# Chunk 0's Gram matrices, its pairs and all decay rows, computed head by head in the projection stage

## The chip, the cores and the metric

The kernel runs on one core of one Trainium2 chip. The metric is the device time of one launch in microseconds (us), lower is better. The engines are TensorE (PE, with its weight loads as PEld), VectorE (DVE), ScalarE (ACT), GpSimd (POOL) and SyncE (SP), which here issues every DMA.

## The reference

One transformer layer in fp32, batch 4, 512 steps, 512 channels, 16 heads of 128, cut to what matters:

```python
q = silu(conv(x @ Wq)); k = silu(conv(x @ Wk)) * 128**-0.5; v = silu(conv(x @ Wv))   # causal, 4 taps
a = sigmoid(x @ Wa + ba); beta = sigmoid(x @ Wb + bb)
def step(St, inp):                       # 512 steps, in order, per batch and head
    err = einsum('bhvk,bhk->bhv', St, k_t) - v_t
    St = a_t[..., None] * St - (b_t[..., None] * err)[..., None] * k_t[:, :, None, :]
    return St, einsum('bhvk,bhk->bhv', St, q_t)
o = layernorm(o) * ln_w + ln_b;  o = (o * sigmoid(x @ Wg)) @ Wo
x = layernorm(x + o);  x = layernorm(x + ternary_ffn(x))
```

The recurrence is solved in 16 chunks of 32 steps. A chunk needs the products k·k of its own steps (the Gram matrices, 32 x 32 for each of the 64 pairs of batch and head), of which only the "pairs" within blocks of 8 steps are used, and the decay over the whole chunk, one row of 128 for each pair of batch and head.

## The kernel before

Five stages follow one another with a barrier between them; the change touches the first two.

**Stage 1, `projections`.** x and the weights are split in a high and a low part, and for each head five matrices are multiplied: A (decay), V, Q, K, G (gate), each in 4 tiles of 128 x 512 (one per batch) with 12 matmuls. Tiles rotate through five of the eight PSUM banks. Per head DVE evicts A, waits for ACT's exponential, scales the `ng` tensor by it, and runs three convolutions (`taps_of`, L424) for V, Q, K. The `ng` tensor is first filled by a broadcast load of beta (L166), which SP issues after the last store of the head before. ACT copies the tiles and makes the silus and the gates. POOL multiplies up decays within blocks of 8 steps (21 steps, semaphore `s_pr`); its last products are `r_out`. DVE splits the weights' low parts (`split`, L419); when the fifth is split (`s_wlo`), SP may load the weights of the next head but one (`weights`, L158). SP works strictly in the order of its list: ng, A, r (2 stores), vt, q, weights, g, k, and then the beta load of the next head. All outputs go to DRAM scratch tensors.

**Stage 2, `recurrence`.** Each of 16 chunks is a cycle. DVE solves a triangular system in 4 blocks for 2 halves of the 64 pairs of batch and head (`solve`, L1173), with `cross` and `start` between. POOL multiplies the pairs by the gates (`with_gates`, L779), masks the key products, decays the state UT (`decay`, L767; needs the decay rows `crow`), rescales X and subtracts v from W (`less_v`). PE transposes X and multiplies. The numbers T_... and D_... are places in a fixed order of the PSUM banks. For chunk c+1 the Gram matrices are made during cycle c: PE `gram` (L984), ACT `copy_gram`, SP `write_gram` to DRAM, then `compact` (7 DRAM to DRAM copies that pick the pairs), then `load_gb` (broadcast to all partitions). Chunk 0 has no cycle before it, so the same chain runs at the head of the stage (L695 to L711, L945 to L953, L1126 to L1141), together with the transposition of all decays into `crow` rows and the first state products, whose state is zero.

**Stages 3 to 5** are the output projection, the ternary weights and the feed-forward net.

Of the kernel before, what the change touches and what calls it, by code (L numbers as in the profile page):

```python
# [5 lines left out]
F32 = mybir.dt.float32  # L6
# [5 lines left out]
P = 128  # L12
# [4 lines left out]
CH = 32  # L17
# [41 lines left out]
def projections(nc, x, w_mats, ba, wb, bb, conv_w, conv_b, scr):  # L59
# [10 lines left out]
    with ExitStack() as ctx:  # L70
# [37 lines left out]
        s_zero = m.sem("zero")  # L108
# [3 lines left out]
        s_exp = m.sem("exp")  # L112
# [6 lines left out]
        s_st = {n: m.sem(f"st_{n}") for n in ("q", "k", "ng", "vt", "A", "g", "r")}  # L119
# [15 lines left out]
        def _(sp):  # L135
# [4 lines left out]
            sp.wait_ge(s_zero, 1)  # L140
# [22 lines left out]
            def head(h, first, left):  # L163
# [9 lines left out]
                store("ng")  # L173
                sp.wait_ge(s_pr, N_PR * (h + 1))
# [4 lines left out]
                sp.wait_ge(s_vt, h + 1)  # L179
                store("vt")  # L180
                sp.wait_ge(s_silu, 3 * h + 2)
                store("q")
# [13 lines left out]
            for n in s_st:  # L196
                sp.wait_ge(s_st[n], (32 if n == "r" else 16) * NH)

        @block.gpsimd
        def _(pool):  # L200
            make_identity(nc, pool, ident, s_id)
            nc.gpsimd.memset(w_in[:, 0, :, :], 0.0).then_inc(s_zero, 1)
            for i in range(2):
                nc.gpsimd.memset(y[i][:, :, 0:KW - 1], 0.0).then_inc(s_zero, 1)
# [9 lines left out]
            def head(h, first):  # L214
# [12 lines left out]
                pool.wait_ge(s_a, h + 1)  # L227
# [36 lines left out]
        def _(act):  # L264
# [18 lines left out]

            def head(h, first, more):
# [31 lines left out]
                nc.scalar.activation(ra[:, :, :], av[:, :, :], ACT.Exp, scale=-1.0).then_inc(s_exp, 1)  # L316
                act.wait_ge(s_exp, h + 1)
                nc.scalar.activation(av[:, :, :], av[:, :, :], ACT.Sigmoid).then_inc(s_a, 1)  # L318
                split(A)
                rows(V)  # L320
                rows(Q)
                silu(V)
                rows(K)
                silu(Q, "q")
                if not first:
                    act.wait_ge(s_st["g"], 16 * h)
                for b in range(B):
                    act.wait_ge(s_mm, TILES * h + PER_MAT * G + b + 1)
                    nc.scalar.activation(outs["g"][:, :, b, :], bank[PER_MAT * G + b][:, :].rearrange("p (c t) -> p c t", t=CH), ACT.Sigmoid).then_inc(s_g, 1)
                split(G)  # L330
                silu(K, "k")
# [7 lines left out]
        def _(pe):  # L339
# [24 lines left out]
            def head(h, first):  # L364
                for mat in range(5):
                    pe.wait_ge(s_wlo, 5 * h + mat + 2)
                    for b in range(B):
# [12 lines left out]
                        product(bank[j][:, :], mat, b).then_inc(s_mm, 1)  # L380

            head(0, True)
            with pe.Fori(1, NH) as h:
                head(h, False)

        @block.vector
        def _(dve):
# [30 lines left out]
            def head(h, first, more):  # L418
# [5 lines left out]
                def taps_of(mat):  # L424
# [5 lines left out]
                    if mat == V:  # L430
                        dve.wait_ge(s_zero, 3)
# [14 lines left out]
                dve.wait_ge(s_exp, h + 1)  # L446
# [27 lines left out]
def weight_piece(views, i, j):  # L474

    return views[i][:, 4 * j:4 * j + 4, :] if i < 2 else views[i][:, j, :, :]


def recurrence(nc, scr, mats, wo, part, res, first):
# [17 lines left out]
    with ExitStack() as ctx:  # L497
# [26 lines left out]
        s_mask = m.sem("mask")  # L524
# [5 lines left out]
        s_cr = m.sem("cr")  # L530
# [25 lines left out]
        T_START, T_CH = 12, 32  # L556
# [18 lines left out]
        all_decays = Gm[:, :, :, :, :].rearrange("p g a i t -> p (g a i t)").rearrange("p (c x) -> p c x", c=NCH)  # L575
        decay_rows = crow[0:HB, 0:NCH, :]
# [12 lines left out]
        def _(sp):  # L589
# [1417 lines left out]
```

## Time and profile before

| | us |
|---|---|
| device time, median of 3 (lowest, highest) | 2773.33 (2772.25, 2779.79) |
| the profiled execution | 2769.04 |
| its span, first to last instruction | 2767.3 |
| PE busy in the span | 2549.2 (92%) |
| DVE busy | 2034.7 (74%) |
| POOL busy | 1415.3 (51%) |
| ACT busy | 1163.7 (42%) |

Stage 1 takes the first 937 us, the recurrence runs from there to about 2022 us. The profiled execution is 1.7 us longer than its span (launch and end) and 4.3 us shorter than the median. Matmul times overlap, so PE's share says how often it had work, not how close it is to its peak.

### The profile page before, as it was taken

The page shows a single profiled execution, that of the slowest core. Times are in us where ns is not written, and L with a number is a line of the kernel's source. Part 1 is how long each engine was busy: PE and PEld are TensorE (multiplying, and loading weights), DVE is VectorE, ACT ScalarE, POOL GpSimd, SP SyncE. Part 2 cuts the span into 40 slices and gives each one's busy share as a digit, 9 for nine tenths or more (in the row PEclk, how much of TensorE's full clock was granted, in tenths as well). Part 3 has the DMA queues.
Part 4 walks back from the last instruction along what each step waited for, and adds up shares of the span by engine and source line. Part 5 has one row for each costly group of instructions (what it writes and reads, how often), then busy time and mean ns, then how long its engine had stood idle before and what let it go on. Part 6 is the DMA issues. An engine that isn't in the chain of part 4 may idle for free. (4 is left out here: it accounts for less than half of the span.)

```text
span 2767.3 us, 50124 instructions
## 1 busy us (share of the span) xinstructions
PE 2549.2 (92%) x17682; PEld 2204.6 (80%) x17682; DVE 2034.7 (74%) x5890; ACT 1163.7 (42%) x2265; POOL 1415.3 (51%) x1213
## 2 busy tenths in 40 slices
PE   8999999999999579999999999999858997899999
PEld 6888878888888569888888888889747776788887
DVE  4777677767777369899999999999769885333333
ACT  4454445444544322222322223323578774333333
POOL 2643554355335489889999988999502220000000
PEclk9999999999999889999999999999869999999999
DMA  5466556555555666555555565566755544000000
GB/s 134 130 164 171 165 144 162 171 168 144 161 168 167 190 240 230 209 199 199 218 200 201 203 232 225 218 235 221 280 205 197 197 167 159 33 11 11 11 11 15
DMA packets 417317, 454.35 MB, mean 164 GB/s; under 512 B 122496, under 2 KB 367232, under 8 KB 393856
## 3 DMA queue, kind: packets, MB, share of 16 engines
q1 hardware_dynamic: 417152, 452.22, 48.7%
q8 instruction: 95, 1.56, 0.2%
q14 instruction: 70, 0.57, 0.1%
HBM read 321.49 MB, written 131.14 MB: 164 GB/s over the span
## 5 line engine op out<-in xcount | busy, mean ns | idle before, releaser
L355 PE MATMUL pa_ps<-pa_x_hi,pa_w_hi 128*128 128x512 f32 x1296 | 508.7, 393 | 10.0 <-ACT pa_y L298 5.6
L355 PE MATMUL pa_ps<-pa_x_lo,pa_w_hi 128*128 128x512 f32 x1296 | 506.0, 390 | 0.0
L355 PE MATMUL pa_ps<-pa_x_hi,pa_w_lo 128*128 128x512 f32 x1296 | 505.7, 390 | 0.0
L438 DVE SCALAR_TENSOR_TENSOR pa_cv<-pa_y,pa_taps,pa_cv 128x2048 f32<-128x2048 f32 x144 | 356.4, 2475 | 17.8
L1188 DVE TENSOR_TENSOR pb_tmp<-pb_gb,pb_ps 128x112 f32<-128x112 f32 (+6 forms) x1792 | 328.8, 222 | 23.6 <-POOL pb_gb L786 19.3
L1193 DVE TENSOR_TENSOR pb_ps<-pb_ps,pb_tmp 128x112 f32<-128x112 f32 (+6 forms) x1792 | 331.2, 227 | 0.0
L786 POOL TENSOR_TENSOR pb_gb<-pb_gb,pb_ng 128x448 f32<-128x448 f32 (+6 forms) x448 | 319.3, 754 | 6.6 <-DMA pb_gb<-scratch_pairs 3.5
L355 PEld LDWEIGHTS pa_ps<-pa_x_hi,pa_w_hi 128*128 128x128 f32 x1296 | 244.2, 188 | 68.6 <-ACT pa_y L298 10.4
L770 POOL TENSOR_TENSOR all_res<-all_res,pb_crow 128x1024 f32<-128x1024 f32 x120 | 282.2, 2363 | 21.2 <-DMA pb_crow<-scratch_crow 21.2
L355 PEld LDWEIGHTS pa_ps<-pa_x_hi,pa_w_lo 128*128 128x128 f32 x1296 | 244.3, 188 | 51.3
L355 PEld LDWEIGHTS pa_ps<-pa_x_lo,pa_w_hi 128*128 128x128 f32 x1296 | 244.4, 189 | 50.0
L1031 PE MATMUL pb_ps<-pb_Gm,pb_XT 128*128 128x64 f32 (+1 forms) x2048 | 251.4, 280 | 6.3 <-DVE all_res L1221 3.1
L1031 PEld LDWEIGHTS pb_ps<-pb_Gm,pb_XT 128*128 128x128 f32 x2048 | 245.2, 198 | 11.6 <-issue 5.9
L225 POOL TENSOR_TENSOR pa_o_vt<-pa_av 128x256 f32<-128x256 f32 x16 | 11.6, 728 | 464.5 <-ACT pa_av L318 464.5
L851 ACT ACTIVATE pb_XT<-pb_ps 128x512 f32<-128x512 f32 x256 | 142.9, 595 | 234.9 <-PE pb_ps L981 234.8
L1006 PE MATMUL pb_ps<-pb_kq,all_res 128*128 128x64 f32 x2048 | 239.6, 277 | 0.0
L1006 PEld LDWEIGHTS pb_ps<-pb_kq,all_res 128*128 128x128 f32 x2048 | 236.6, 195 | 0.7
L873 ACT ACTIVATE pb_Gm<-pb_ps 128x256 f32<-128x256 f32 (+1 forms) x256 | 77.3, 354 | 334.0 <-PE pb_ps L997 334.0
L981 PE MATMUL pb_ps<-pb_ident,pb_X 128*128 128x128 f32 x1024 | 150.6, 287 | 71.9 <-DVE pb_X L1201 55.3
L1898 DVE SCALAR_TENSOR_TENSOR pe_hid<-pe_ps,all_scales,pe_sil 128x512 f32<-128x512 f32 x64 | 48.1, 751 | 227.9 <-ACT pe_sil L1782 227.9
L981 PEld LDWEIGHTS pb_ps<-pb_ident,pb_X 128*128 128x128 f32 x1024 | 115.7, 146 | 95.9 <-DVE pb_X L1201 78.1
L452 DVE SCALAR_TENSOR_TENSOR pa_o_ng<-pa_ra,pa_o_ng 128x512 f32<-128x512 f32 x64 | 72.9, 1197 | 129.4 <-DMA pa_o_ng<-scratch_beta 129.4
(192 smaller groups left out, 5364.8 us busy)
## 6 DMA issues: line engine op xcount, KB each, us to landing
pb_crow<-scratch_crow SPq DMA_DIRECT2D x30, 2048.0 KB, 10.2
pb_gb<-scratch_pairs SPq DMA_DIRECT2D x64, 896.0 KB, 8.2
pa_o_ng<-scratch_beta SPq DMA_DIRECT2D x16, 1024.0 KB, 7.9
scratch_ng<-pa_o_ng SPq DMA_DIRECT2D x16, 1024.0 KB, 4.5
scratch_A<-pa_o_A SPq DMA_DIRECT2D x16, 1024.0 KB, 4.5
scratch_vt<-pa_o_vt SPq DMA_DIRECT2D x16, 1024.0 KB, 4.5
scratch_q<-pa_o_q SPq DMA_DIRECT2D x16, 1024.0 KB, 6.9
scratch_g<-pa_o_g SPq DMA_DIRECT2D x16, 1024.0 KB, 8.1
```

What stands on the lines that cost most here:

```text
L355: last = nc.tensor.matmul(out, w[:, mat, k, :], xx[:, k, b * S:(b + 1) * S], start=(k == 0 and n == 0), stop=(k == KT - 1 and n == 2))
L438: nc.vector.scalar_tensor_tensor(out=out, in0=yy[:, :, k:k + S], scalar=tap(k), in1=out, op0=ALU.mult, op1=ALU.add).then_inc(s_tap, 1)
L452: last = nc.vector.scalar_tensor_tensor(out=out, in0=tile(ra, b), scalar=-1.0 / DV, in1=out, op0=ALU.mult, op1=ALU.mult)
L770: tt(uu, uu, crow[:, 8 * (e % 4):8 * (e % 4) + 8, :], ALU.mult).then_inc(s_us, 1)
L786: last = tt(pairs, pairs, ng[:, :, BL * n + t:BL * n + t + 1].broadcast_to([P, HB, w]), ALU.mult)
L851: nc.scalar.activation(out, psT[j % 2][:, :].rearrange("p (g k) -> p g k", g=4), ACT.Copy).then_inc(s_te, by)
L873: last = nc.scalar.activation(Gm[:, g:g + 4, a, :, steps], src[:, :, 1 - a, :, part], ACT.Copy)
L981: last = nc.tensor.transpose(bank[:, q * P:(q + 1) * P], src, ident[:, :])
L1006: last = nc.tensor.matmul(bank[:, 64 * q:64 * q + 64].rearrange("p (a t) -> p a t", a=2), UT[:, 8 * j + q, :], kq[p][:, :, 8 * j + q, :], ...
L1031: last = nc.tensor.matmul(bank[:, 64 * q:64 * q + 32 * kinds].rearrange("p (a i t) -> p a i t", i=4, t=BL), XT[:, g, :], Gm[:, g, 0:kinds, ...
L1188: tt(tmp[:, hs, 0:w], gb[n][:, hs, off[t]:off[t] + w], ys[:, qs, t:t + 1].broadcast_to([P, QUART, w]), ALU.mult).then_inc(s_sv, 1)
L1193: tt(ys[:, qs, t + 1:BL], ys[:, qs, t + 1:BL], tmp[:, hs, 0:w], ALU.add).then_inc(done, 1)
```

## The change

In stage 1, Q and K change places: K is now the third matrix and Q the fourth, and the stores likewise (k early, q last). Behind the fifth matrix of each head PE multiplies the 4 Gram matrices of chunk 0 for this head and transposes its decays of all chunks (`grams`), into a sixth PSUM bank; ACT copies both out (`gram_out`) and SP stores them (`store_gram`, `store_decays`). In the last head this happens ahead of the last tile, and SP also runs the compaction of chunk 0 there. The recurrence then starts with loads alone. The decay rows lie in DRAM by head and then by chunk, so that a load of half of them reads 8 runs per partition instead of one. The zero fills of the state and of the first half of W, O and y are made by DVE, in place of POOL's fill and of the first products with the zero state; PE's bank counter starts at 4 instead of 12. The file also renames a few semaphores (`s_exp`, `s_zero` and `s_mask` are folded into others).

```diff
@@ projections: SP
+                def store_gram():
+                    sp.wait_ge(s_gk, 2 * h + 2)
+                    sp.dma_start(scr["gram"][0, 0:CH * HB * CH].rearrange("(j h x) -> h j x", j=CH, h=NH)[h, :, :], gk[0:CH, 0:P]).then_inc(s_st["gram"], 16)
+                def store_decays():
+                    sp.dma_start(scr["crow"][h, :, :, :].rearrange("c b v -> (c b) v"), gk[:, P:2 * P]).then_inc(s_st["gram"], 16)
+                if left == 0:
+                    sp.wait_ge(s_silu, 3 * h + 2)
+                    store("k")
                 sp.wait_ge(s_pr, N_PR * (h + 1))
                 store("A")
...
+                if left == 0:
+                    store_gram()
+                    sp.wait_ge(s_vt, h + 1)
+                    store("vt")
+                    sp.wait_ge(s_st["gram"], 32 * NH - 16)
+                        compact_pairs(sp, scr, 0, s_st["gram"])
+                if left:
+                    sp.wait_ge(s_vt, h + 1)
+                    store("vt")
+                    sp.wait_ge(s_silu, 3 * h + 2)
+                    store("k")
                 if left >= 2:
                     weights(h + 2)
                 sp.wait_ge(s_g, 4 * h + 8)
                 store("g")
+                if left:
+                    store_gram()
+                store_decays()
                 sp.wait_ge(s_silu, 3 * h + 3)
-                store("k")
+                store("q")
@@ projections: GpSimd
+                    pool.wait_ge(s_gr, h)
@@ projections: ScalarE
+            def gram_out(h, first):
+                act.wait_ge(s_gr, h + 1)
+                if not first:
+                    act.wait_ge(s_st["gram"], 32 * h)
+                nc.scalar.activation(gk[0:CH, 0:P], gram[0:CH, 0:P], ACT.Copy).then_inc(s_gk, 1)
+                nc.scalar.activation(gk[:, P:2 * P], gram[0:NCH * B, P:2 * P], ACT.Copy).then_inc(s_gk, 1)
@@ projections: TensorE
+            def grams(h, first):
+                pe.wait_ge(s_pr, N_PR * (h + 1))
+                pe.wait_ge(s_silu, 3 * h + 2)
+                if not first:
+                    pe.wait_ge(s_gk, 2 * h)
+                for b in range(B):
+                    k = outs["k"][:, 0, b, :]
+                    nc.tensor.matmul(gram[0:CH, CH * b:CH * (b + 1)], k, k, start=True, stop=True)
+                decays = r_out[:, 1, :, :, NBL - 1].rearrange("p c b -> p (c b)")
+                nc.tensor.transpose(gram[0:NCH * B, P:2 * P], decays, ident[:, :]).then_inc(s_gr, 1)
...
                         product(bank[j][:, :], mat, b).then_inc(s_mm, 1)
+                        if mat == G and b == (B - 1 if more else B - 2):
+                            grams(h, first)
@@ recurrence: SP
-                sp.dma_start(flat(crow[:, :, :]), scr["crow"][c, HALF * hf:HALF * (hf + 1), :].rearrange("h v -> (h v)").partition_broadcast(P)).then_inc(s_crl, 16)
+                sp.dma_start(crow[:, :, :].rearrange("p (h b) v -> p h (b v)", b=B),
+                             scr["crow"][NH // 2 * hf:NH // 2 * (hf + 1), c, :, :].rearrange("h b v -> h (b v)").partition_broadcast(P)).then_inc(s_crl, 16)
@@ recurrence: GpSimd
-            nc.gpsimd.memset(UT[:, :, :], 0.0).then_inc(s_te, 4)
-            nc.gpsimd.memset(O[1][:, :, :], 0.0).then_inc(s_os[1], 16)
+            nc.gpsimd.memset(O[1][:, 0:1, :], 0.0).then_inc(s_os[1], 16)
...
-            for hf in range(2):
-                masked(8 + 2 * hf + 1, 0, hf)
             with_gates(0, 0)
+            masked(1, 0, 0)
             with_gates(0, 1)
+            masked(3, 0, 1)
@@ recurrence: VectorE
-            for j in range(4):
-                start(D_START - D_CH, 0, j, 3 if j == 3 else 1)
+            nc.vector.memset(UT[:, 0:HALF, :], 0.0).then_inc(s_dp, 6)
+            nc.vector.memset(UT[:, HALF:HB, :], 0.0).then_inc(s_te, 4)
+            nc.vector.memset(W[:, 0:HALF, :], 0.0)
+            nc.vector.memset(O[0][:, 0:HALF, :], 0.0)
+            nc.vector.memset(y_of[0], 0.0).then_inc(s_de, 6)
             first_v(D_START - D_CH, 0, 0)
```

`compact_pairs` is the old body of `compact`, moved out so that both stages call it. In DVE's list of stage 1 the convolution of K takes the place of Q's, and Q's the last place.

**SP in the loop over heads of stage 1**, from the store of vt to the end of the body. Before:

```order
L170 DMA scratch_vt<-pa_o_vt 128x16x128
L170 DMA scratch_q<-pa_o_q 128x16x128
L161 DMA pa_w_in<-in_Wa 128x4x128
L161 DMA pa_w_in<-in_Wv 128x4x128
L161 DMA pa_w_in<-in_Wq 128x4x128
L161 DMA pa_w_in<-in_Wk 128x4x128
L161 DMA pa_w_in<-in_Wg 128x4x128
L170 DMA scratch_g<-pa_o_g 128x16x128
L170 DMA scratch_k<-pa_o_k 128x16x128
```

Now:

```order
L172 DMA scratch_vt<-pa_o_vt 128x16x128
L172 DMA scratch_k<-pa_o_k 128x16x128
L163 DMA pa_w_in<-in_Wa 128x4x128
L163 DMA pa_w_in<-in_Wv 128x4x128
L163 DMA pa_w_in<-in_Wk 128x4x128
L163 DMA pa_w_in<-in_Wq 128x4x128
L163 DMA pa_w_in<-in_Wg 128x4x128
L172 DMA scratch_g<-pa_o_g 128x16x128
L178 DMA scratch_gram<-pa_gk 32x128
L181 DMA scratch_crow<-pa_gk 64x128
L172 DMA scratch_q<-pa_o_q 128x16x128
```

Two small stores now stand between the store of g and the last store of the head, and so ahead of the beta load that opens the next pass.

**SP from the last head into the recurrence.** Before (the last two stores, the barrier at L70, and the chain of chunk 0):

```order
L170 DMA scratch_g<-pa_o_g 128x16x128
L170 DMA scratch_k<-pa_o_k 128x16x128
L70 UNCONDITIONAL_BRANCH
L588 UNCONDITIONAL_BRANCH
L591 DMA pb_kq<-scratch_k 128x2048
L591 DMA pb_kq<-scratch_q 128x2048
L599 DMA pb_rr<-scratch_r 128x256 x2
L697 DMA pb_Gm<-scratch_r 128x16x256
L607 DMA scratch_gram<-pb_gst 32x512 x4
L591 DMA first_A<-scratch_vt 128x2048
L619 DMA scratch_pairs<-scratch_gram 256x1x7
```

Now, from the end of the compaction in the last head:

```order
L537 DMA scratch_pairs<-scratch_gram 256x1x1
L172 DMA scratch_g<-pa_o_g 128x16x128
L181 DMA scratch_crow<-pa_gk 64x128
L172 DMA scratch_q<-pa_o_q 128x16x128
L70 UNCONDITIONAL_BRANCH
L646 UNCONDITIONAL_BRANCH
L677 DMA pb_gb<-scratch_pairs 128x1792
L649 DMA pb_ng<-scratch_ng 128x2048
L649 DMA first_A<-scratch_vt 128x2048
L649 DMA pb_kq<-scratch_k 128x2048
L649 DMA pb_kq<-scratch_q 128x2048
L657 DMA pb_rr<-scratch_r 128x256 x2
```

The seven compaction copies stand ahead of the barrier (L70), and the first load behind it is that of the pairs (`gb`); k and q come fourth and fifth.

**PE at the head of the recurrence.** Before:

```order
L989 MATMUL pb_ps<-pb_kq 32x32 x64
L1006 MATMUL pb_ps<-pb_kq,all_res 128x64 x32
L1137 MATMUL pb_ps<-pb_ident,pb_Gm 64x128 x16
L997 MATMUL pb_ps<-pb_kq 128x128 x16
L981 MATMUL pb_ps<-pb_ident,pb_X 128x128 x8
```

Now:

```order
L1039 MATMUL pb_ps<-pb_kq 128x128 x16
L1023 MATMUL pb_ps<-pb_ident,pb_X 128x128 x8
L1039 MATMUL pb_ps<-pb_kq 128x128 x4
L1073 MATMUL pb_ps<-pb_Gm,pb_XT 128x64 x8
L1039 MATMUL pb_ps<-pb_kq 128x128 x4
L1031 MATMUL pb_ps<-pb_kq 32x32 x48
```

The Gram products (L989), the state products (L1006) and the transposes of the decays (L1137) are gone from here; the key products (now L1039) come first. The last row, the Gram matrices of chunk 1, waits for chunk 1's k and q.

## Rows read from the trace of the kernel before

**Rows 1.** The page, part 5: a convolution step of DVE, busy us and mean ns.

```profile
L438 DVE SCALAR_TENSOR_TENSOR pa_cv<-pa_y,pa_taps,pa_cv 128x2048 f32<-128x2048 f32 x144 | 356.4, 2475 | 17.8
```

**Rows 2.** Waits of PE in stage 1: us in total, times, longest.

```profile
PE pa_ps L355 <- ACT pa_y L298: 5.6, 9, 0.8
```

**Rows 3.** Timeline of DVE, one head: start us, us, instruction, idle before.

```profile
822.97 2.72 DVE L444 TENSOR_SCALAR pa_av<-pa_ps,pa_ba_sb 128x512 f32<-128x512 f32 x4
...
839.15 4.87 DVE L452 SCALAR_TENSOR_TENSOR pa_o_ng<-pa_ra,pa_o_ng 128x512 f32<-128x512 f32 x4 [8.84 <-DMA pa_o_ng<-scratch_beta]
...
878.15 2.72 DVE L444 TENSOR_SCALAR pa_av<-pa_ps,pa_ba_sb 128x512 f32<-128x512 f32 x4
```

**Rows 4.** Timeline of SP, the same head.

```profile
823.22 0.40 SPq L161 DMA_DIRECT2D pa_w_in<-in_Wa  x1
...
826.23 0.40 SPq L170 DMA_DIRECT2D scratch_g<-pa_o_g  x1
826.81 3.82 SPq L170 DMA_DIRECT2D scratch_k<-pa_o_k  x1
830.84 2.78 SPq L166 DMA_DIRECT2D pa_o_ng<-scratch_beta  x1
```

**Rows 5.** Windows, that head: engines' busy us, PEclk, DMA share, GB/s.

```profile
828.00:829.00 1.00, 1.00 (x6) 0.84 (x5) 0.00 (x0) 1.00 (x1) 0.00 (x0) 1.00 0.86 229
...
831.00:832.00 1.00, 1.00 (x6) 0.84 (x5) 0.00 (x0) 1.00 (x1) 0.00 (x0) 1.00 1.14 346
```

**Rows 6.** Timeline of PE: decay transposes, and Gram products of a later chunk.

```profile
959.62 1.14 PE L1137 MATMUL pb_ps<-pb_ident,pb_Gm 128*64 128x128 f32 x8 [0.24 <-ACT pb_crow L950]
...
998.25 1.20 PE L989 MATMUL pb_ps<-pb_kq 128*32 128x32 f32 x32
```

**Rows 7.** Timeline, end of stage 1 and first load of the recurrence.

```profile
916.93 0.30 POOL L256 COPY pa_r_out<-pa_r_out 128x64 f32<-128x64 f32 x1
...
917.26 0.37 SPq L170 DMA_DIRECT2D scratch_A<-pa_o_A  x1
...
917.67 3.94 SPq L177 DMA_DIRECT2D scratch_r<-pa_r_out  x2
...
930.23 0.39 SPq L170 DMA_DIRECT2D scratch_k<-pa_o_k  x1
...
937.10 0.35 SPq L591 DMA_DIRECT2D pb_kq<-scratch_k  x1
```

**Rows 8.** Timeline, head of the recurrence.

```profile
938.16 6.92 POOL L739 MEMSET all_res<- 128x8192 f32 x1
...
954.75 6.51 SPq L619 DMA_DIRECT2D scratch_pairs<-scratch_gram  x7
...
963.75 3.88 POOL L765 TENSOR_TENSOR pb_Gm<-pb_Gm,pb_mask 128x512 f32<-128x512 f32 x4 [13.19 <-ACT pb_Gm L873]
...
971.17 9.89 POOL L786 TENSOR_TENSOR pb_gb<-pb_gb,pb_ng 128x448 f32<-128x448 f32 x14 [3.54 <-DMA pb_gb<-scratch_pairs]
...
976.23 0.45 DVE L1188 TENSOR_TENSOR pb_tmp<-pb_gb,pb_ps 128x112 f32<-128x112 f32 x2 [16.33 <-POOL pb_gb L786]
...
981.00 1.82 POOL L777 TENSOR_TENSOR pb_W<-pb_W,first_A 128x768 f32<-128x768 f32 x1
...
982.63 2.07 PE L997 MATMUL pb_ps<-pb_kq 128*128 128x128 f32 x8
...
989.18 0.45 DVE L1188 TENSOR_TENSOR pb_tmp<-pb_gb,pb_ps 128x112 f32<-128x112 f32 x2
...
1002.39 0.45 DVE L1188 TENSOR_TENSOR pb_tmp<-pb_gb,pb_ps 128x112 f32<-128x112 f32 x2 [2.94 <-POOL pb_gb L786]
```

**Rows 9.** Window of the first loads (columns as in rows 5).

```profile
940.00:945.00 5.00, 0.00 (x0) 0.00 (x0) 0.00 (x0) 0.00 (x0) 5.00 (x1) 0.50 1.01 400
```

**Rows 10.** DMA issues of 900 to 1010 us: KB each, median us to landing.

```profile
scratch_gram<-pb_gst SPq DMA_DIRECT2D x8, 64.0 KB, 2.1
```

**Rows 11.** Waits of POOL from the recurrence on.

```profile
POOL all_res L770 <- DMA pb_crow<-scratch_crow: 21.2, 14, 6.6
```

More of the change, by code:

```diff
@@ L178, in head @@
                                  r_out[:, i, :, :, :].rearrange("p n b k -> p n (b k)")).then_inc(s_st["r"], 16)
[L179 to L182, printed above, removed]
+                if left == 0:
[3 more added lines that the diff above has]
+                    sp.wait_ge(s_st["gram"], 32 * NH - 16)
+                    with nc.allow_non_contiguous_dma(reason="compaction to the pairs, chunk 0"):
+                        compact_pairs(sp, scr, 0, s_st["gram"])
[4 more added lines that the diff above has]
+                    store("k")
                 if left >= 2:
@@ L327, in head @@
                 for b in range(B):
+                    if b == B - 1 and not more:
+                        gram_out(h, first)
                     act.wait_ge(s_mm, TILES * h + PER_MAT * G + b + 1)
                     nc.scalar.activation(outs["g"][:, :, b, :], bank[PER_MAT * G + b][:, :].rearrange("p (c t) -> p c t", t=CH), ACT.Sigmoid).then_inc(s_g, 1)
+                if more:
+                    gram_out(h, first)
                 split(G)
-                silu(K, "k")
+                silu(Q, "q")
             head(0, True, True)
@@ L362, in _, with head @@
             pe.wait_ge(s_beta, B)
-            def head(h, first):
+            def grams(h, first):
[8 more added lines that the diff above has]
+                nc.tensor.transpose(gram[0:NCH * B, P:2 * P], decays, ident[:, :]).then_inc(s_gr, 1)
+            def head(h, first, more):
                 for mat in range(5):
@@ L476, in weight_piece, with compact_pairs @@
     return views[i][:, 4 * j:4 * j + 4, :] if i < 2 else views[i][:, j, :, :]
+def compact_pairs(sp, scr, c, sem):
+    row = HB * CH
+    off = [sum(BL - 1 - i for i in range(j)) for j in range(BL)]
+    for j in range(BL - 1):
+        first = j * row + j + 1
+        src = scr["gram"][c, first:first + NBL * (BL * row + BL)].rearrange("(n s) -> n s", n=NBL)[:, 0:row]
+        sp.dma_start(scr["pairs"][c, :, :, off[j]:off[j + 1]],
+                     src.rearrange("n (h t) -> n h t", t=CH)[:, :, 0:BL - 1 - j]).then_inc(sem, 16)
 def recurrence(nc, scr, mats, wo, part, res, first):
@@ L612, in compact @@
                 for k in range(2):
-                    sp.wait_ge(s_gw[k], 32 * (c + 1))
-                row = HB * CH
+                    sp.wait_ge(s_gw[k], 32 * c)
                 with nc.allow_non_contiguous_dma(reason="compaction to the pairs, once per chunk"):
-                    for j in range(BL - 1):
-                        first = j * row + j + 1
-                        src = scr["gram"][c, first:first + NBL * (BL * row + BL)].rearrange("(n s) -> n s", n=NBL)[:, 0:row]
-                        sp.dma_start(scr["pairs"][c, :, :, off[j]:off[j + 1]],
-                                     src.rearrange("n (h t) -> n h t", t=CH)[:, :, 0:BL - 1 - j]).then_inc(s_gc, 16)
+                    compact_pairs(sp, scr, c, s_gc)
             def load_gb(c, n):
```

126 lines of the change are left out of this document (52 added, 74 removed).

## The prediction, made before the changed kernel ran

> **What bounds the kernel now.** I read the timeline of each engine over one head of stage 1, then the waits, the windows of the DMA engines, and the timeline across the barrier into the recurrence.
>
> In stage 1 PE looks like the bound, but in at least nine of the sixteen heads it waits 0.6 us for a tile that ACT could not yet copy (5.6 us in 9 waits) [rows 2]. So something else sets the pace by a small margin. DVE shows what: it begins two heads 55.18 us apart (822.97 and 878.15), and between them it stands idle for 8.84 us until the beta load for `ng` lands; from 839.15 to the next head it is never free for long [rows 3]. SP shows why the load is late. It may load weights only when DVE has split the fifth matrix, at about 823. Then come five weight loads, the store of g at 826.23, the store of k at 826.81 and the beta load at 830.84 [rows 4]. So the loop is: 39.0 us of DVE (839.15 to 878.15), then 16.2 us of SP's list and the DMA engines (822.97 to 839.15). At its head the DMA engines are short of work (229 GB/s at 828), afterwards full (346 GB/s at 831) [rows 5].
>
> At the end of stage 1 the last store is issued at 930.23 and the recurrence opens at 937.10 [rows 7]. I call 937.10 S. From there DVE waits until 976.23, S+39.1, for the pairs of chunk 0, which POOL multiplies from 971.17 [rows 8]. The whole chain of Gram matrices, stores and compaction lies ahead of that. The second block begins at S+52.1 (989.18), the third at S+65.3 (1002.39) [rows 8].
>
> **The change, part by part.**
>
> *PE in stage 1.* Sixteen Gram products took 1.20 us (32 records, two for each), so four are 0.30 us; eight transposes took 1.14 us, so one is 0.14 [rows 6]. That is 0.44 us a head, 7.1 in all. PE's waits of 0.6 us cover it as long as the DVE loop sets the pace [rows 2]. I take 0, with 0 and 7 as bounds. The new wait for POOL's products costs nothing in the loop. In the last head POOL ends at 917.2 [rows 7], and the Gram products stand behind the third G tile; what they hold up is one tile's gate, while DVE's convolution runs until some 2 us before the last store. ACT's two copies lie in its idle time.
>
> *Two small stores in SP's list.* They stand before the last store of the head and thus before the beta load. Issue to issue is 0.58 us (826.23 to 826.81) [rows 4], so two cost SP 1.16 us. But SP's next store is then held up by full queues (3.82 us), and g's 1 MB keeps the engines fed meanwhile. Only their 48 KB are certain: 0.14 us at 346 GB/s [rows 5]. Since the engines are not quite full just there, I take 0.25 us a head, 3.5 us over the 14 passes through this loop; the bounds are 2 and 16.
>
> *The end of stage 1.* K's 1 MB now leaves before A's store, which takes 3.0 us of backlog away (1 MB at 346). But SP must do this in order: r's two stores until 921.6 [rows 7], the Gram store, then wait for its landing, 2.1 us when little is queued [rows 10] and some 4 us behind A and r, so about 926. Seven compaction copies took 6.51 us [rows 8]; I count 5 to 6.5. Then g, the decays and q at 0.58 each: q is issued at 932.5 to 934 in place of 930.23. With two full stores still to move (6.1 us at 346) the barrier opens at about 940. I take +3, bounds 0 and +6.
>
> *The head of the recurrence.* Loads run at 400 GB/s [rows 9], with some 2.5 us before the first lands. The order is gb (0.9 MB), ng, vt, k, q (1 MB each), rr, gb, crow (2 MB), two gb, and chunk 1's k and q, 12.3 MB in all. So ng lands at S+7.4, q at S+15.3, crow at S+23.5 and chunk 1's q at S+33.
> - POOL, now without the fill of 6.92 us [rows 8], starts the gates at S+7.4. Half of 9.89 us later [rows 8], at S+12.4, the pairs are ready.
> - DVE fills 10,496 elements per partition. No row has a DVE fill; POOL's took 0.84 ns an element [rows 8], a convolution step on DVE 1.21 ns [rows 1]. That gives 8.9 to 12.7 us and with y minus v a start at S+10.3 to S+14.1. I take S+12.8, near POOL's rate. Solving takes 4.5 us, to S+17.3.
> - PE's four key products wait for q. Four of them as at 982.63, 2.07 us each, are 8.3 us [rows 8]; that was after an idle stretch. The granted clock is 0.50, the lower level of 1.2 GHz, over the first loads, when PE has done nothing for a while, and 1.00 amid stage 1 [rows 5, 9]. At the low level they end at S+23.6, at the full one (half the time) at S+19.5; I take S+22. The rest of the step (12.95 us from solve to solve, less 4.5 for the solve) is 8.4 us: S+30.4.
> - POOL masks the first half behind the key products (half of 3.88 us, to S+22), makes the second gates (4.95, S+27), masks again (1.9) and subtracts v (1.82) [rows 8]: S+30.8. DVE adds this in 0.4 and begins block 2 at about S+31.3, against S+52.1.
> - Then POOL's list up to the third gates is as before, 19.6 us from 982.8 (981.00 + 1.82), of which some 6.6 were the wait for crow [rows 11], which now lies in SBUF. So the third block starts near S+43.9 in place of S+65.3. PE's Gram products of chunk 1 wait for S+33 and delay it by about 1 us.
>
> The gain is thus 21 to 21.4 us at these points, 20.5 with PE's lateness. Lower bound 16: everything at 346 GB/s, the slow clock and the slow fill. Upper bound 22.
>
> The Trainium skill, "DMA: Bandwidth & Descriptors", section "Where 436 GB/s comes from", puts the limit of one core's HBM at about 358 GB/s. By that limit 12.3 MB would take 34.4 us in place of 30.8, and the gain would be about 18 us. The window shows 400 [rows 9], so the sum stays with the row.
>
> *Decay rows in 2 KB runs.* Rows show 346 GB/s for runs of 512 bytes and 400 for long ones [rows 5, 9], so a load of 2.1 MB grows by at most 0.8 us. POOL waited 14 times for crow, 21.2 us in all [rows 11], but PE makes it wait behind that as well, and DVE does not wait for it. I take +1 in all, bounds 0 and 12.
>
> **The sum**, against the profiled execution of 2769.04: -20.5 + 3.5 + 3 + 1 = -13.0, that is 2756. The median of the runs shown is 4.3 above that execution, 2773.33, so I forecast 2760.
>
> **The rivals.**
>
> *A: SP's issue time is paid in full.* For it: SP's list is the loop's link, and the engines run short at 828 [rows 5]. Against: the store behind is held up for 3.82 us anyway [rows 4]. 1.16 x 14 = 16.2 us in place of 3.5, so 2773: no change. Chance 0.14.
>
> *B: the gain at the head is smaller, or PE's products are not hidden.* If PE stays at the low clock and chunk 1's loads come late, the gain is 13 and the time 2768; if the 7.1 us of PE are paid, 2767. For it: PE has idled before and the list puts k and q fourth and fifth. Against: before, POOL and not PE set the third block [rows 8]. Chance 0.15.
>
> *C: slower. Each small store holds up the beta load by its full landing time*, 2.1 us [rows 10]. Place: between g and q in SP's list, each head. Price: 4.2 x 14 = 59 us in place of 3.5, so 2816. It decides as soon as a head grows by over 1.2 us (16.5 us over 14 heads); past 1.8 us it is measurably slower. For it: this list is the bound. Against: SP does not wait for a landing there, and other stores overlap. Chance 0.09. Beside it stands a rule of the Trainium skill, "DMA: Bandwidth & Descriptors", section "Anatomy of one DMA": a DMA has a fixed cost of some 2.0 us whatever its size. The landing of 2.1 us for 64 KB agrees with it, and the same section puts most of that in the completion, which would not add up here.
>
> *The forecast*, stage 1 growing by little and 17 to 22 us won at the head: 0.62.
>
> **How the numbers follow.** What a measurement of this kernel can tell is about 0.3%, 8.3 us, so 2765 and 2782 divide the cases. The forecast case lies from 2751 to 2765, B mostly within 0.3%, A within, C above. That gives faster 0.63, same 0.27, slower 0.10. The range 2750 to 2776 holds the forecast, B and A and leaves out C and the ends of both sides, some 0.18.
>
> **What would show it.** Right: the distance between two heads on DVE at 55.3 to 55.6 us; PE's waits in stage 1 shorter than 0.6; the barrier 5 to 8 us later than 937.1; the first solve at 12 to 15 us behind the first load of the recurrence, the second block at 30 to 33, the third at 43 to 46; crow waits of POOL 0.5 us longer in each chunk, and chunks as long as before. Wrong: a distance of 56.3 or more between heads (A, C), POOL or PE late in the first chunk (B), or a compaction that ends after 933 at the end of stage 1.

## The result: 2821 us, slower by about 2%

| | median us (lowest, highest; runs) | ratio to before, 95% interval |
|---|---|---|
| before, beside it | 2772.79 (2771.44, 2779.79; 4) | |
| changed | 2821.10 (2815.41, 2835.01; 4) | 1.0205 [1.0166, 1.0244] |

2760 with 2750 to 2776 was predicted. The quotient of the two medians alone is 1.0174, inside the interval. That the kernel is slower is clear; whether by 2% is open. The profiled execution is the slowest of the four, 2835.01 us with a span of 2833.3, against 2769.04 for that of before. So the traces differ by 66 us where the medians differ by 48.

The timeline up to the recurrence reads almost as predicted. DVE, two heads of stage 1 (as in [rows 3]):

```profile
825.10 2.72 DVE L495 TENSOR_SCALAR pa_av<-pa_ps,pa_ba_sb 128x512 f32<-128x512 f32 x4
...
880.85 2.72 DVE L495 TENSOR_SCALAR pa_av<-pa_ps,pa_ba_sb 128x512 f32<-128x512 f32 x4
```

The distance is 55.75 us in place of 55.18; the last head begins 2.7 us later than before. SP at the end of the stage (as in [rows 7]):

```profile
925.30 0.89 SPq L178 DMA_DIRECT2D scratch_gram<-pa_gk  x1
...
928.67 5.26 SPq L537 DMA_DIRECT2D scratch_pairs<-scratch_gram  x7
...
936.91 0.59 SPq L172 DMA_DIRECT2D scratch_q<-pa_o_q  x1
943.22 0.34 SPq L677 DMA_DIRECT2D pb_gb<-scratch_pairs  x1
```

S is now 943.22, 6.1 us later. The head of the recurrence (as in [rows 8]):

```profile
944.14 3.47 DVE L1293 MEMSET all_res<- 128x4096 f32 x1 [13.22 <-PEq L70]
...
950.64 4.97 POOL L833 TENSOR_TENSOR pb_gb<-pb_gb,pb_ng 128x448 f32<-128x448 f32 x7 [2.51 <-DMA pb_ng<-scratch_ng]
...
955.72 0.45 DVE L1219 TENSOR_TENSOR pb_tmp<-pb_gb,pb_ps 128x112 f32<-128x112 f32 x2 [0.81 <-POOL pb_gb L833]
...
958.31 5.91 PE L1039 MATMUL pb_ps<-pb_kq 128*128 128x128 f32 x32 [32.44 <-DMA pb_kq<-scratch_q]
...
973.87 0.45 DVE L1219 TENSOR_TENSOR pb_tmp<-pb_gb,pb_ps 128x112 f32<-128x112 f32 x2
...
981.32 1.91 PE L1031 MATMUL pb_ps<-pb_kq 128*32 128x32 f32 x32 [12.12 <-DMA pb_kq<-scratch_q]
...
993.36 0.45 DVE L1219 TENSOR_TENSOR pb_tmp<-pb_gb,pb_ps 128x112 f32<-128x112 f32 x2
```

Gates at S+7.4, solve at S+12.5, second block at S+30.7: all three as in the sum. Only then something is late: chunk 1's q is there at S+38.1 in place of S+33, and the third block at S+50.1 in place of S+43.9. The windows say why. While the decay rows load, the DMA engines move less (columns as in rows 5):

```profile
960.00:965.00 5.00, 4.83 (x31) 4.59 (x31) 0.25 (x1) 2.40 (x9) 2.27 (x3) 0.73 0.74 244
965.00:970.00 5.00, 4.21 (x36) 3.92 (x35) 0.75 (x2) 2.23 (x6) 5.00 (x8) 1.00 0.63 153
```

The same loads in `e1_rows_by_chunk` (below), where the decay rows lie in one run, keep their rate:

```profile
955.00:960.00 5.00, 4.81 (x35) 4.49 (x34) 0.16 (x1) 2.71 (x9) 2.42 (x3) 0.82 0.98 414
960.00:965.00 5.00, 3.69 (x33) 3.50 (x32) 0.75 (x2) 1.91 (x5) 5.00 (x8) 1.00 1.02 423
```

All 30 loads of the decay rows are slow. DMA issues (KB each, median us to landing), before and after:

```profile
pb_crow<-scratch_crow SPq DMA_DIRECT2D x30, 2048.0 KB, 10.2
```

```profile
pb_crow<-scratch_crow SPq DMA_DIRECT2D x30, 2048.0 KB, 16.7
```

These medians hide a pattern. Before, the loads land alternately after some 8.6 and 13.6 us, and the median falls between the two; in the changed kernel both kinds take 15 to 19 us (the first 25). By the mean without the first load the growth is from 10.9 to 16.6 us. POOL's wait for them grew from 21.2 us [rows 11] to 130.3. Waits of POOL, and one of them on its timeline:

```profile
POOL all_res L817 <- DMA pb_crow<-scratch_crow: 130.3, 24, 9.9
```

```profile
1018.41 2.36 POOL L817 TENSOR_TENSOR all_res<-all_res,pb_crow 128x1024 f32<-128x1024 f32 x1 [9.93 <-DMA pb_crow<-scratch_crow]
```

A chunk can be measured by ACT's instruction that occurs once in each. First and last after:

```profile
993.91 0.61 ACT L972 ACTIVATE pb_ngx<-pb_ng 128x512 f32<-128x512 f32 x1
...
2025.88 0.64 ACT L972 ACTIVATE pb_ngx<-pb_ng 128x512 f32<-128x512 f32 x1
```

That is 1031.97 us for 15 distances, 68.8 us each; before (L925, from 1000.04 to 1960.72) they are 64.05. So the account of the profiled executions is: the first of these instructions comes 6.1 us earlier than before, 15 x 4.75 = 71.3 us are lost, and the last comes 65.2 us later; under 1 us of the 66 lies behind it. The surprise is in the chunks and in 6 us of the head, both behind the loads of the decay rows.

### The profile page after: what moved, and what is told of

The parts are those of the page before. It is cut to its first block and busy times, and to the rows that moved or that the text cites. A ratio compares the mean times of both kernels' runs of the same rounds, so it can differ in the third digit from the quotient of the medians.

```text
span 2833.3 us, 50183 instructions
## 1 busy us (share of the span) xinstructions
PE 2599.8 (92%) x17618; PEld 2253.7 (80%) x17618; DVE 2041.6 (72%) x5883; ACT 1166.3 (41%) x2289; POOL 1398.4 (49%) x1212
## 5 line engine op out<-in xcount | busy, mean ns | idle before, releaser
L817 POOL TENSOR_TENSOR all_res<-all_res,pb_crow 128x1024 f32<-128x1024 f32 x120 | 282.3, 2364 | 130.3 <-DMA pb_crow<-scratch_crow 130.3
L391 PEld LDWEIGHTS pa_ps<-pa_x_lo,pa_w_hi 128*128 128x128 f32 x1296 | 244.2, 188 | 50.1
L1073 PE MATMUL pb_ps<-pb_Gm,pb_XT 128*128 128x64 f32 (+1 forms) x2048 | 263.7, 288 | 21.1 <-issue 9.3
L1073 PEld LDWEIGHTS pb_ps<-pb_Gm,pb_XT 128*128 128x128 f32 x2048 | 257.4, 206 | 28.1 <-issue 20.6
L1048 PE MATMUL pb_ps<-pb_kq,all_res 128*128 128x64 f32 x1984 | 254.6, 293 | 0.0
L1048 PEld LDWEIGHTS pb_ps<-pb_kq,all_res 128*128 128x128 f32 x1984 | 252.5, 211 | 0.6
L248 POOL TENSOR_TENSOR pa_o_vt<-pa_av 128x256 f32<-128x256 f32 x16 | 11.7, 730 | 473.8 <-ACT pa_av L350 473.8
L1039 PE MATMUL pb_ps<-pb_kq 128*128 128x128 f32 x1024 | 163.1, 309 | 39.7 <-DMA pb_kq<-scratch_q 32.4
## 6 DMA issues: line engine op xcount, KB each, us to landing
pb_crow<-scratch_crow SPq DMA_DIRECT2D x30, 2048.0 KB, 16.7
```

The lines of the kernel that those rows point to most:

```text
L391: last = nc.tensor.matmul(out, w[:, mat, k, :], xx[:, k, b * S:(b + 1) * S], start=(k == 0 and n == 0), stop=(k == KT - 1 and n == 2))
L817: tt(uu, uu, crow[:, 8 * (e % 4):8 * (e % 4) + 8, :], ALU.mult).then_inc(s_us, 1)
L1039: last = nc.tensor.matmul(bank[:, q * P:(q + 1) * P].rearrange("p (a i t) -> p a i t", a=2, i=4), flat(kq[p][:, 0, 4 * g:4 * g + 4, :]), k ...
L1048: last = nc.tensor.matmul(bank[:, 64 * q:64 * q + 64].rearrange("p (a t) -> p a t", a=2), UT[:, 8 * j + q, :], kq[p][:, :, 8 * j + q, :], ...
L1073: last = nc.tensor.matmul(bank[:, 64 * q:64 * q + 32 * kinds].rearrange("p (a i t) -> p a i t", i=4, t=BL), XT[:, g, :], Gm[:, g, 0:kinds, ...
```

## The experiments

The chunk times below are means over the first 14 of these distances unless said otherwise; after has 68.75 by this measure. Landing is the median of the 30 loads of the decay rows.

**Is it the layout?** `e1_rows_by_chunk` is the changed kernel with the decay rows in DRAM by chunk, one run of 16 KB for each partition; each head's store then scatters its rows.

```diff
-sp.dma_start(scr["crow"][h, :, :, :].rearrange("c b v -> (c b) v"), gk[:, P:2 * P])
+sp.dma_start(scr["crow"].rearrange("c (g b) v -> g c b v", b=B)[h, :, :, :], gk[:, P:2 * P])
...
```

The tensor's shape and the load are those of the kernel before; these two lines are left out here.

> The changed kernel, but the decay rows lie in DRAM by chunk again, so that a load of half of them reads one run of 16 KB per partition. Theory L (the layout of the decay rows makes their loads slow, and this alone makes the recurrence longer): loads land in about 10 us in place of 16.7, POOL waits about 20 us for them in all in place of 130, chunks follow each other at about 63.7 us, and the time falls from 2821 to about 2760. Theory O (the loads are slow because of their place among the others, or the chunks are slow because the first one is out of step): the landing stays above 14 us and the time above 2800.

Measured: 2760.09 us, ratio 0.9955 [0.9928, 0.9982]; landing 11.3 us, POOL's waits 15.3 us. `e2_before_rows_by_head` is the kernel before with only the layout of the change (and 16 stores in place of one to write it).

> The kernel before, with one thing of the change alone: the decay rows lie in DRAM by head and then by chunk (written by 16 small stores in place of one), and a load reads 8 runs of 2 KB, 32 KB apart. Theory L: the loads land in about 16.7 us, POOL waits over 100 us for them, and the time rises by 60 to 70 us to about 2835. Theory O: the time stays within 10 us of 2773.

Measured: 2840.41 us, 1.0236 [1.0183, 1.0289]; landing 16.6 us, POOL's waits 147.7 us, chunks 68.4 us. Not all of its +71 us is the layout's: SP issues the 16 stores in 15.37 us where the one took 1.38, and this kernel's third block begins 10.6 us further behind S than that of the kernel before, which is the stores and the slow first load together. Its chunks grew by 4.2 us, nearly as in the changed kernel. So the layout makes the loss in the chunks with or without the rest of the change, and without it (e1) the time is 2760 us.

**Short runs or their distance?** The prediction had thought of the length of the runs (2 KB) only. These kernels keep runs of 2 KB, eight for each partition, and change how far apart they lie. `e3_pitch_34k` leaves one chunk's room free behind each head:

```diff
-"scratch_crow", (NH, NCH, B, P)
+"scratch_crow", (NH, NCH + 1, B, P)
```

> The changed kernel with one chunk of padding behind each head's decay rows, so that the 8 runs of 2 KB of a load lie 34 KB apart and not 32 KB. Theory P (the distance, a power of two, puts all 8 runs on the same part of the HBM): the landing falls to about 10.5 us and the time to 2765. Theory R (runs of 2 KB are slow to read for 128 partitions at once, whatever their distance): landing 16 to 17 us and time 2815 to 2825, as in the changed kernel.

`e4_pitch_2k5` sorts by chunk and head, with a gap of one row of 512 bytes behind each run (`(NCH, NH, B + 1, P)`).

> The changed kernel with the decay rows by chunk, but 512 bytes of padding behind each head's 2 KB: 8 runs of 2 KB, 2.5 KB apart, all within 20 KB. Theory P: landing about 10.5 us, time about 2765. Theory R: landing 16 to 17 us, time 2815 to 2825.

`e5_pitch_4k` and `e6_pitch_16k` put the heads inside groups of 2 and 8 chunks (`(NCH // 8, NH, 8, B, P)` for the latter), `e7_pitch_64k` leaves half of each head's room free (`(NH, 2 * NCH, B, P)`), and `e8_pitch_33k` two rows of it (`(NH, NCH * B + 2, P)`).

> The changed kernel, the runs of a load 4 KB apart. If any power of two as distance slows the load: landing near 16.7 us, time near 2820. If only large distances do (eight runs that fall on the same few places of the memory): landing 11 to 12 us, time 2755 to 2762. I expect something between or the second.

> The same with 16 KB between the runs. If distances of 32 KB and more are the bad ones: landing 11 to 12 us, time 2755 to 2762. If the slowness grows by steps with the distance: landing 13 to 15 us, time 2775 to 2800. I expect the second.

> The same with 64 KB between the runs. If the distance counts by its power of two: as bad as 32 KB or worse, landing 16 to 20 us, time 2815 to 2850. If 32 KB alone were bad by an accident of where the tensor lies: landing 11 to 12 us and 2755 to 2762.

> The same with 33 KB between the runs, the smallest step off 32 KB here. If 1 KB more is enough to spread the runs: landing 11 to 12 us, time 2753 to 2762. If it takes the 2 KB of the run itself: landing 13 to 16 us, time 2775 to 2815.

| distance of the runs | landing us | POOL's waits us | time us | ratio |
|---|---|---|---|---|
| one run of 16 KB (e1) | 11.3 | 15.3 | 2760.09 | 0.9955 [0.9928, 0.9982] |
| 2.5 KB (e4) | 11.7 | 26.3 | 2755.16 | 0.9958 [0.9921, 0.9994] |
| 4 KB (e5) | 11.9 | 52.2 | 2758.36 | 0.9956 [0.9925, 0.9987] |
| 16 KB (e6) | 16.8 | 135.2 | 2830.98 | 1.0216 [1.0079, 1.0353] |
| 32 KB (changed kernel) | 16.7 | 130.3 | 2821.10 | 1.0205 [1.0166, 1.0244] |
| 33 KB (e8) | 11.6 | 24.6 | 2754.49 | 0.9962 [0.993, 0.9993] |
| 34 KB (e3) | 11.7 | 20.1 | 2753.38 | 0.9942 [0.9912, 0.9971] |
| 64 KB (e7) | 15.1 | 79.2 | 2767.38 | 0.9997 [0.9967, 1.0027] |

The landings and waits are of one execution each. The length of the runs costs some 0.4 us a load (11.7 against 11.3), as the prediction's 0.8 allowed. The distance costs five more. I had expected 16 KB to lie between, and it is as bad as 32; I had expected 64 KB to be as bad or worse, and it is milder. One KB beside 32 KB is enough to undo all of it. So it is the exact distance and not its size. A distance of 4 KB is a power of two as well and is harmless; 8 KB was not run. What in the memory coincides at 16, 32 and 64 KB no trace here shows. The Trainium skill, "DMA: Bandwidth & Descriptors", section "Latency and other measured facts", tells of copies of whole tiles whose rate falls from 207 GB/s at a row distance of 512 KB to 164 at 2 MB and 103 at 4 and 8 MB, and is back at 214 with 4 KB more than 4 MB. It names the collision of memory channels as an inference only. The runs here agree in kind, at a far smaller distance, within one partition's data, and with 1 KB as padding.

The 64 KB row also shows where the slack ends: 3.4 us more per load than at 34 KB cost 14 us in all, the next 1.6 us more than 50. The median hides why: at 64 KB the loads still alternate, 11.8 and 17.7 us (at 34 KB 9.1 and 13.6), while at 16 and 32 KB both kinds take some 16 to 17. What costs most is that the early kind becomes late too.

**How do the later landings become 4.7 us per chunk?** (4.5 by the first 14 distances, for which before has 64.21.) The wait is in POOL, two loads per chunk, 130.3 - 21.2 = 109 us more over 30 loads. Windows of single chunks show two kinds of growth (from one ACT instruction to the next; columns as in rows 5). After:

```profile
1470.75:1545.03 74.28, 69.33 (x655) 65.21 (x655) 59.88 (x300) 18.74 (x42) 62.89 (x56) 0.85 0.61 185
1752.56:1817.71 65.15, 59.47 (x658) 55.53 (x657) 58.62 (x292) 18.67 (x42) 53.58 (x49) 1.00 0.75 211
```

And two of e1, the kernel by chunk:

```profile
1821.13:1884.36 63.23, 59.56 (x658) 55.78 (x657) 59.06 (x295) 18.66 (x42) 57.33 (x53) 1.00 0.58 218
1174.12:1243.86 69.74, 66.08 (x658) 62.29 (x658) 59.18 (x296) 18.68 (x43) 56.59 (x52) 0.90 0.53 197
```

In the kernel by chunk 63.2 us is the usual chunk at a granted clock of 1.00. In the changed kernel the only chunk at 1.00 takes 65.15; the others, at 0.85 to 0.97, take 66 to 74. Counted in windows of 2 us over some 970 us, the granted clock fell below 0.9 15 times in the changed kernel and 6 times in e1 (the kernel before has 5). What PE did before a fall (timeline, then windows of PE's busy time and clock):

```profile
1499.87 1.97 PE L1073 MATMUL pb_ps<-pb_Gm,pb_XT 128*128 128x64 f32 x16 [1.50 <-POOL pb_Gm L812]
...
1503.18 6.93 PE L1048 MATMUL pb_ps<-pb_kq,all_res 128*128 128x64 f32 x32
```

```profile
1498.00:1501.00 3.00, 1.50 (x18) 1.34 (x15) 2.17 (x4) 0.00 (x0) 3.00 (x3) 1.00 1.04 429
...
1504.00:1507.00 3.00, 3.00 (x16) 3.00 (x15) 3.00 (x23) 0.00 (x0) 3.00 (x3) 0.50 0.98 410
```

The decay rows came 8.78 us late to POOL, its masks behind them were late for PE, PE stood for 1.50 us, and then its 32 products ran at 0.50, the lower level of 1.2 GHz. That looked like a second loss on top of the wait. To test it, `e9_change_pe_filled` lets PE multiply tiles that nobody needs where it waits for X (a table of fillers that L1054 reads, all zero until now):

```diff
-FILL = [0, 0, 0, 0, 0, 0, 0, 0]
+FILL = [2, 2, 2, 2, 2, 2, 2, 2]
```

> The changed kernel as it is, with its bad layout, but PE multiplies two tiles that nobody needs ahead of each of the eight groups of X transposes of a chunk, mostly where it waits for DVE. Theory: only about 2 us of the 4.7 us that a chunk grew is the wait for the decay rows; the rest is that PE, waiting more often, falls to the lower clock (in the recurrence of the changed kernel the chunks at a granted clock of 1.00 take 65.2 us, those at 0.85 to 0.93 take 67 to 74). If so, the filled PE keeps a granted clock near 0.99, chunks take 65 to 66.5 us, time 2775 to 2800. Rival: the lower clock is only a reflection of the idle time and costs nothing; then the added products cost up to 3 us a chunk and the time is 2820 to 2865.

Measured: 2828.21 us, 1.0176 [1.0115, 1.0237]; chunks 68.75 us as before, granted clock 0.95 after 0.93, 13 falls. No gain, but also hardly a test: the falls remained, seven of them within some 3 us of a wait of PE ahead of L1073, where it needs the masks; this filler doesn't cover it. `e10_by_chunk_pe_filled` has the same filler in the kernel by chunk.

> The same filler in the kernel with the decay rows by chunk, where two of fourteen chunks fell to 0.90 and took 69.7 us in place of 63.2. If the filler prevents these dips: chunks at 63.2 to 64 us throughout, 2745 to 2758. If it costs more than it gives: 2765 to 2800.

Measured: 2754.33 us, 0.9943 [0.9922, 0.9965]; two falls, chunks of 63.6 us with hardly an exception (the last of the 15 took 68.3 at 0.90), between 2750.66 and 2757.77 in all seven runs. `e13_change_filled_at_masks` puts filler also ahead of the masks in the changed kernel:

```diff
 bank = bank_d(at_d, d)
+if n == 1:
+    busy(bank, 6)
 pe.wait_ge(s_te, at + T_X[hf][n] + 2 + 4)
 pe.wait_ge(s_gm[hf], 4 * c + 2 * min(n, 1) + 2)
```

> The changed kernel with its bad layout and the filler of the ninth run, and besides that six tiles that nobody needs (about 1.3 us) ahead of the products of block 1 of each half, where PE waits for masks that POOL multiplies late behind the decay rows. In the ninth run seven of the thirteen falls of the granted clock came within 3 us of just that wait. If idle time there makes the clock fall, and the fall a good part of the loss: granted clock in the recurrence at 0.97 to 1.00 in place of 0.93, chunks 65.5 to 66.5 us, time 2785 to 2800. If the falls come anyway, or cost nothing: 2820 to 2860.

Measured: 2838.86 us, 1.0255 [1.0202, 1.0307]. The clock came back, to 0.98 in place of 0.93; the time did not. `e15_by_chunk_filled_at_masks` is its control in the kernel by chunk.

> The thirteenth run's filler in the kernel with the decay rows by chunk, as its control. In the bad layout this filler brought the clock back (chunks at 0.95 to 1.00), and yet the chunks stayed at 69.1 us. If the added tiles cost nearly nothing in the good layout (chunks at 63.6 to 64.5 us, 2752 to 2770), then the clock's falls were no loss of their own, and the whole 4.7 us of a chunk is the late decay rows. If they cost their 2.6 us (chunks near 66 us, 2785 to 2800), the filler took back what the clock gave, and the falls stand for some 2.6 us of a chunk.

Measured: 2785.31 us, 1.0065 [1.004, 1.009]. The windows over 14 chunks, after, e13 and e15:

```profile
993.91:1956.45 962.54, 892.06 (x9170) 836.92 (x9169) 827.62 (x4116) 262.41 (x575) 799.54 (x728) 0.93 0.69 199
```

```profile
993.04:1960.16 967.12, 911.18 (x9465) 824.91 (x9561) 828.00 (x4116) 260.11 (x576) 798.35 (x728) 0.98 0.69 198
```

```profile
984.29:1907.46 923.17, 890.01 (x9464) 809.98 (x9561) 826.48 (x4116) 260.01 (x575) 805.95 (x730) 1.00 0.55 208
```

With equal filler the layout costs 69.1 - 65.9 = 3.1 us a chunk, at a clock of 0.98 against 1.00. The filler itself costs 65.9 - 63.2 = 2.7 us in the kernel by chunk. If it costs the same in the changed one, a chunk there would take 69.1 - 2.7 = 66.4 us at a clock of 0.98, and the measured 68.75 would hold 2.3 us more for their lower clock of 0.93, against 64.4 - 63.2 = 1.2 in e1. So of the growth from 64.4 to 68.75, 4.3 us, the late data make 1.9 (65.15 - 63.23) to 3.1 us and the lower clock the rest. The lower end has more chunks for it than one: at a clock of 1.00 one chunk of e2 takes 65.38 us and one of e9 65.26, and the six such chunks of e13 have a mean of 67.7, 1.7 above e15's. Still this split is an estimate over differences of single executions, and the chunks at 1.00 may be those with the least late data. Shown is that this filler raises the clock and wins no time back; that it costs as much as the clock gives is the likely reason and rests on the price in e15.

**What does a small store in SP's list cost?** `e11_six_small_stores` adds four stores like the two of the change in each pass of the loop, to a place that nobody reads, with the rows by chunk.

> Rows by chunk, and six small stores in each pass of the loop over heads in place of two (the four added ones write the same data to a place that nobody reads). This prices what two of them cost. By my sum (0.25 us for two): the distance of two heads on DVE grows from 55.7 to 56.3 us at most, time 2758 to 2768. If SP's issue time is paid in full (0.58 us each): 58.0 us a head, time 2790 to 2795. If each costs its landing: over 64 us a head, time above 2870.

Measured: 2768.69 us, 0.9995 [0.9971, 1.0019]. DVE's heads:

```profile
832.86 2.72 DVE L502 TENSOR_SCALAR pa_av<-pa_ps,pa_ba_sb 128x512 f32<-128x512 f32 x4
889.26 2.72 DVE L502 TENSOR_SCALAR pa_av<-pa_ps,pa_ba_sb 128x512 f32<-128x512 f32 x4
```

Over the last six distances the means are 55.44 us before, 55.47 in e1 with two small stores, and 56.29 in e11 with six: 0.2 us for each of the four added, a third of SP's issue time. But the slack is not where it seems. DVE's step that waits for the beta load (`pa_o_ng`) begins 16.7 us behind the head's start before, 16.7 in the changed kernel, 16.6 in e1 and 19.0 in e11 (means over the last seven heads). So two stores delay the beta load by nothing that shows, and four more delay it by 2.4 us, their full issue time of 0.6 us each. The rest of DVE's head then took 37.3 us in place of 38.8; why, no run shows. Rival A is refuted for two stores, and its price would be right at the beta load for the next four.

**A better head.** `e12_head_order` takes the kernel by chunk, loads k and q of chunk 0 ahead of v, k and q of chunk 1 ahead of the last two gates' pairs, and lets PE multiply 24 filler tiles from the start.

```diff
@@ recurrence: SP
-load(vt[:, :, :], "vt", 0, s_vl)
 load_kq(0, 0)
-load_rr(0, 0)
+load(vt[:, :, :], "vt", 0, s_vl)
 load_gb(0, 1)
+load_rr(0, 0)
 load_crow(0, 0)
+load_kq(1, 1)
 load_gb(0, 2)
 load_gb(0, 3)
-load_kq(1, 1)
@@ recurrence: TensorE
+busy(psT[0], 24)
 pe.wait_ge(s_te, 4)
```

> Rows by chunk, and another order of the loads at the head of the recurrence: k and q of chunk 0 before v, k and q of chunk 1 before the last two gates' pairs, and PE multiplies 24 tiles that nobody needs while it waits. Expected: key products at S+13 in place of S+15.1, second block at S+27 in place of S+30.6, chunk 1's Gram products without a wait, third block at S+40 in place of S+44; time 2 to 4 us below the kernel with rows by chunk, which one measurement can hardly tell. Rival: the first solve waits for v instead and the second block stays at S+30.

Measured: 2752.70 us, 0.9933 [0.9888, 0.9977]. The stage opens at 940.94 (SP's first load):

```profile
940.94 0.34 SPq L676 DMA_DIRECT2D pb_gb<-scratch_pairs  x1
```

```profile
953.35 5.44 PE L1038 MATMUL pb_ps<-pb_kq 128*128 128x128 f32 x32 [3.23 <-issue]
...
968.98 1.20 PE L1030 MATMUL pb_ps<-pb_kq 128*32 128x32 f32 x32 [1.73 <-DMA pb_kq<-scratch_q]
```

The key products start at S+12.4, the second block at S+27.1, the third at S+39.8 (DVE at 968.02 and 980.78), all within 1 us of the expectation. The rest of it came only in part: the first solve waits for v and begins at S+15.3, in e1 at S+12.5, and chunk 1's Gram products still waited 1.73 us. In this execution the gain did not last either. Right behind the third block PE's 64 products with the state took 13.92 us at a granted clock of 0.50 (7.36 in e1), and the fourth block began at S+55.8, in e1 at S+52.6. In e14 it began at S+49.2. `e14_head_order_pe_filled` joins the three edits, by chunk, this order, and the filler of e10.

> The three edits that stand so far in one kernel: decay rows by chunk, the new order at the head of the recurrence, the filler ahead of the X transposes. If they add: third block at S+40, chunks at 63.6 us with no or one dip, 2747 to 2752 with a narrower spread than the others. If the filler's 0.35 us a chunk eats what the steadier clock gives: 2752 to 2757, no better than one of them alone.

Measured: 2750.57 us (2745.56 to 2765.65, 12 runs), 0.9943 [0.9915, 0.997], granted clock 0.975 over the span, against 0.945 of the changed kernel. Leaving out the two with additions that cost time (e11, e15), all kernels with a harmless distance lie between 0.9933 and 0.9962 with intervals that overlap: each beats the kernel before, by some 0.5%, and which of them is the best no run here can tell.

## Why the prediction was wrong

**The step that failed** is the last of the sum, "Decay rows in 2 KB runs": "a load of 2.1 MB grows by at most 0.8 us ... I take +1 in all, bounds 0 and 12". A load grew by 6.5 us in the median (10.2 to 16.7) and by 5.6 in the mean, and the term was not +1 but +61 between the medians of the changed kernel and e1, and some +75 between their profiled executions. Its bound came from rows that vary the length of the runs [rows 5, 9]; none varied their distance, though the layout of the change puts the runs 32 KB apart. Part of the step was right: length alone costs under a microsecond (e3, e4, e8). The other half of it, that DVE "does not wait" for crow, failed as well. POOL multiplies masks behind the decay, PE waits for the masks, and DVE for PE.

**The other terms held in size, not all of them by the mechanism that was given.**
- Two small stores, +3.5: the last head began 2.7 us late in the profiled execution, but one execution does not settle this. In the fourteen kernels with two such stores the last head begins between 876.1 and 881.9 us (mean 879.0), and in the two without at 876.5 (e2) and 878.15. Rival A (each paid in full) and rival C (each its landing) did not come: in the changed kernel and in e1 the distance of two heads stayed under 56.3 from the third on, and the beta load was not later.
- PE's 0.44 us a head at 0: this may be where the growth came from. Windows from the second head to the last, before and after:

```profile
100.45:878.15 777.70, 771.95 (x3385) 633.38 (x3384) 582.59 (x421) 378.02 (x435) 377.55 (x294) 1.00 0.57 162
```

```profile
99.91:880.85 780.94, 777.99 (x3509) 639.78 (x3508) 581.82 (x422) 383.12 (x463) 370.90 (x294) 1.00 0.58 162
```

PE worked 6.0 us longer (first number behind the length), its waits for ACT took up 2.6 of them (5.6 us before, 3.0 after), and the rest is nearly the growth of 3.2 us. The prediction set 0.44 us a head against waits of 0.6, but only nine heads had one, and in these 777.7 us PE had 5.7 to spare. So PE's products can explain the growth without any cost of the stores; no run adds the products alone, and the split stays open.
- End of stage 1, +3: 6.1 us in all at S, less 2.7, is 3.4. From the last head to S all fourteen kernels take 62.1 to 63.9 us, against 58.95 before. The compaction took 5.26 us, inside the 5 to 6.5.
- The head, -20.5: the first 31 us of it are within 1 us of the forecast. With the layout mended (e1) the third block is at 982.10 - 938.13 = S+44.0 for S+43.9, a gain of 21.3 at that block. In the changed kernel the slow load of the decay rows stood ahead of chunk 1's q and took 6 us of it. Rival B (slow clock, late loads) describes this delay, but not its cause.
- DVE's fill, bounded by 0.84 and 1.21 ns an element: 3.47 us for 4096, 0.85.
- The sum without the failed term: 2760 was forecast, e1 gave 2760.09 with the kernel before at 2768.98 beside it. Against its own neighbour that is a gain of 9 us in the medians, not 13; e1's interval allows 5 to 20. So the gain agrees within the noise, and that the time itself hits to 0.1 us is luck.

None of the rivals held the cause. The slower one (C) had a time near the measured one, 2816, but by a mechanism that the trace refutes; the range missed because no case let a load become slow. The section of the Trainium skill that stands beside it ("DMA: Bandwidth & Descriptors", "Anatomy of one DMA") speaks of DMAs that GpSimd issues, and these are SP's; the row's landing of 2.1 us needs no page.

## What to carry to other kernels

When a layout in DRAM changes, look at the distance between the runs that one load reads, not only at their length, and treat an unpriced distance of 16 KB or a larger power of two as a risk with its own bound; one or two KB of padding cost nothing here and gave some 60 us. Look at single landings too, since a median over two kinds of loads can hide which kind became late. Before a term is put at nothing because an engine has waits, add up those waits: 5.6 us could not hide 7.1. A side tensor of 2 MB per load can be a bound although it is prefetched: ask how late it may land before its reader's queue is late for the engine behind. If a change is slow, first run the kernel before with one part of it; that run (e2), with the change without that part beside it (e1), named the culprit.

## What was not expected of the hardware

- Broadcast loads of eight 2 KB runs: landing 16.8 us at 16 KB distance, 16.7 at 32 KB, 15.1 at 64 KB, but 11.6 at 33 KB and 11.9 at 4 KB.
- In e1 six of fourteen chunks take 63.2 to 63.3 us, and two 69.7 at a granted clock of 0.90. Two fillers before each group of transposes (e10) cost 0.35 us a chunk, and of the fourteen none took more than 64.9.
- Filler that raises the granted clock from 0.93 to 0.98 can leave the time where it was (e13).
